# Mixture attention: VectorE's maxima one head ahead, ScalarE's exponentials ahead of the high halves

## The chip, the cores and the metric

One core of a Trainium2 chip runs the whole program. The metric is the device time of that core in microseconds (us), from launch to end; the profile's span, from the first instruction to the last, is a little shorter.

## The reference

A two-layer decoder over 8 batches of 256 tokens of width 256: layer 0 is a gated cross attention, then a gated mixture-attention layer; layer 1 a gated cross attention, then a mixture of 12 experts. The change touches only the mixture attention:

```python
q = einsum('btc,hdc->bhtd', x, Wq);  k = einsum('btc,hdc->bhtd', x, Wk)      # 16 heads of 64
w, sel = top_k(einsum('btc,hec->bthe', x, Ws), 2)                            # 2 of 8 value experts
mix_v = one-hot(sel) weighted by sigmoid(w)
v = einsum('bthe,bted->bhtd', mix_v, einsum('btc,edc->bted', x, Wv))
attn = softmax(q @ k.T / 8) @ v                                              # per batch and head
mask_o = two-hot of top_k(einsum('btc,hec->bthe', x, Wd), 2)                 # 2 of 8 output experts
res = einsum('bthe,bthd,efd->btf', mask_o, attn, Wo)
```

x is layer-normed first, and the result is added to x with a gate. No causal mask, so a head's scores are 256 x 256.

## The kernel before, in words

Every engine runs one instruction stream in order and meets the others at counting semaphores. Matrix products are taken in fp16 with each factor split into a high and a low half (three products, `matmul3`, lines 82 to 84). Splitting a product that lies in PSUM takes two engines: ScalarE copies the high half out, then VectorE subtracts it and writes the low half, which frees the bank.

The stage (`ffn_stage`, line 899) walks 8 batches b with 16 steps h each (one head a step), and a drain of 16 steps. In step h of batch b:

- TensorE (line 1326): transposes of the exponentials of head h-1 (L1225), value products of head h-3, one *product* of the next batch's front (`project(b + 1, h)`), then `score(b, h + 2)`. After the score, at steps 9 and 12 it does the mix-back of the batch before (`mixed_back`, L1309), and at 11 and 14 its output product. The front's products are, by step: 0 the transposes of x, 1 the gates, 2 and 3 the expert values, 4 to 10 and 15 queries and keys in turn, 11 to 14 the mixed values.
- ScalarE (line 1181): the high half of the transposed exponentials of head h-2 (`pt_part`), the high half of the product of step h-1 (`high`), then the exponentials of head h (`exps`, L1154), and in odd steps the normalising of a finished pair of heads (`normalise`). At step 4 it also converts the heads' outputs (`heads_hi`), at steps 10 and 13 the high half of a mix-back (`back_hi`).
- VectorE (line 1478): the maxima of head h (`maxima`, L1437), at h = 0 the normalised x of the next batch, the low half of `pt_part`, in odd steps reciprocals of row sums, the low half of the product of step h-1 (`low`, `low_x`), and then the extras: gate choice in five parts (steps 2 to 6), the heads' low halves (step 4), the spread of output masks (7, 8), of mixed values (10 to 13), low halves of the mix-back (10, 13), updates of x (12, 15).

Two score banks S alternate by head. `score(n)` waits until the exponentials of head n-2 have left its bank; `maxima(n)` waits for `score(n)` and for the exponentials of n-2, whose maxima it overwrites; `exps(n)` waits for `maxima(n)` and for the transposes of n-2. Two more banks hold, in turn, everything of the front, the mix-back and the output product, in the order that `bank_uses` lists; each use waits (`open_bank`, line 1257) until the use two before it has been released by VectorE. The gates product waits for the low half of x.

The other stages, among them the cross attentions and the experts, are not touched. GpSimd and SP serve the stage with row copies and DMA round trips.

Of the kernel before, what the change touches and what calls it, by code (L numbers as in the profile page):

```python
# [35 lines left out]
B, SQ, D = 8, 256, 256  # L36
SK = 120
H = 16
# [855 lines left out]
def at_head(h):  # L894

    return h % H8, h // H8


def ffn_stage(nc, a, s):
# [7 lines left out]
    with ExitStack() as ctx:  # L907
# [65 lines left out]
        def earlier(b, h, lag, do):  # L973

            if h >= lag and b < B:
                do(b, h - lag)
            elif h < lag and b >= 1:
                do(b - 1, h - lag + H)
# [138 lines left out]
        @block.scalar  # L1117
        def _(act):
            def pt_part(b, h):
                n = H * b + h  # L1120
                act.wait_ge(pt_ready, n + 1)
                if n >= 2:
                    act.wait_ge(pv_done, n - 1)
                act.activation(pt[h % 2][:, 0].rearrange("p c t q -> p (c t q)"), PT(h), ACT.Copy,  # L1124
                               scale=SPLIT).then_inc(pt_hi, 1)

            def high(b, j):
                use = b, FF_ORDER[j]
                what, r = use[1]
                act.wait_ge(front_ready, USE[use] + 1)  # L1130
                front = bank(use)
                if what == F_XN:
                    ins = act.activation(xt[b % 2][:, 0].rearrange("p c q -> p (c q)"), front, ACT.Copy, scale=SPLIT)
                elif what == F_GATES:
                    act.activation(g[:].rearrange("p a e -> p (a e)"), front, ACT.Copy, scale=UNSPLIT)
                    act.activation(mix[:], front.rearrange("p (t v h e) -> p t v h e", t=TPB, v=2, h=H)[:, :, 0],
                                   ACT.Exp, scale=-UNSPLIT).then_inc(act_high, 1)
                    return
                else:
                    if what == F_PV and r == 0 and b >= 1:  # L1140
                        act.wait_ge(pv_out, 16 * b)
                    if what == F_MIXV and r % 2 == 0 and b >= 1:
                        act.wait_ge(v_out[r // 2], 16 * b)
                    to, _, scale = parts_of(use)
                    ins = act.activation(to, front.rearrange("p (a c) -> p a c", a=to.shape[1]), ACT.Copy, scale=scale)
                ins.then_inc(act_high, 1)

            def exps(b, h):
                n = H * b + h
                act.wait_ge(s_max, n + 1)  # L1150
                if n >= 2:
                    act.wait_ge(pt_ready, n - 1)
                for ti in range(TPB):
                    ins = act.activation(pr[h % 2][:, ti, :], S(h)[:, ti, :], ACT.Exp, bias=nb[h % 2][:, ti:ti + 1])  # L1154
                ins.then_inc(p_ready, 1)

            def normalise(b, hp):
                h = 2 * hp
                act.wait_ge(rs_done, H // 2 * b + hp + 1)
                for i in range(2):  # L1160
                    h8, x = at_head(h + i)
                    for ti in range(TPB):
                        ins = act.activation(at[:, ti, h8, x, :], O(h)[:, i, ti, 0:DH], ACT.Copy,
                                             scale=rs[hp % 2][:, 2 * i + ti:2 * i + ti + 1])
                ins.then_inc(o_done, 1)

            def heads_hi(b, ti):
                act.wait_ge(o_done, H // 2 * (b + 1))
                if b >= 1:
                    act.wait_ge(at_out[ti], 16 * b)  # L1170
                act.activation(at_row[:, ti, :, 0:DH], at[:, ti].rearrange("p h x d -> p (h x) d"), ACT.Copy).then_inc(at_hi, 1)

            def back_hi(b, ti):
                use = b, (F_Z, ti)
                act.wait_ge(front_ready, USE[use] + 1)
                act.activation(zt[:, 0].rearrange("p c q -> p (c q)"), bank(use), ACT.Copy).then_inc(act_high, 1)

            act.wait_ge(made, 6)
            for j in range(FF_FRONT - 1):
                high(0, j)  # L1180
            for b in range(B + 1):
                for h in range(H):
                    earlier(b, h, FF_LAG - 1, pt_part)
                    was = (b, FF_FRONT - 1) if h == 0 else (b + 1, h - 1)
                    if was[0] < B:
                        high(*was)
                    for ti in range(TPB):
                        if b >= 1 and h == SPLIT_STEPS[ti]:
                            back_hi(b - 1, ti)
                        if b >= 1 and h == HEADS_STEPS[ti]:  # L1190
                            heads_hi(b - 1, ti)
                    if b < B:
                        exps(b, h)
                    if h % 2 == 1:
                        if h >= 5 and b < B:
                            normalise(b, (h - 5) // 2)
                        elif h < 5 and b >= 1:
                            normalise(b - 1, (h - 5) // 2 + H // 2)
# [148 lines left out]
        def _(dve):  # L1347
# [53 lines left out]
            def spread_values(b, r):  # L1401

                if r == 0:
                    dve.wait_ge(mix_in, 16 * (b + 1))
                if r >= 2:
                    dve.wait_ge(front_ready, USE[b, (F_MIXV, r - 2)] + 1)
                elif b >= 1:
                    dve.wait_ge(front_ready, USE[b - 1, (F_MIXV, r + 2)] + 1)
                n = SPREAD * 4
                dve.tensor_tensor(spread_v[r % 2][:].rearrange("p g l t h -> p (g l) t h"),  # L1410
                                  mix_in_t[:, SPREAD * r:SPREAD * r + SPREAD].rearrange("p g l h -> p (g l) h")
                                  .unsqueeze(2).to_broadcast([P, n, TG, H8]),
                                  same[:].unsqueeze(1).to_broadcast([P, n, TG, H8]), ALU.mult).then_inc(v_spread, 1)
# [54 lines left out]
            for j in range(FF_FRONT - 1):  # L1468
                if j == 0:
                    low_x(0)  # L1470
                low(0, j)
                if j == 1:
                    dve.wait_ge(act_high, HIGH[0, (F_GATES, 0)] + 1)
                if j in GATE_STEPS:
                    gate_choice(GATE_STEPS.index(j))
                if j + 1 in VALUE_STEPS:
                    spread_values(0, VALUE_STEPS.index(j + 1))
            for b in range(B + 1):
                for h in range(H):
                    if b < B:  # L1480
                        maxima(b, h)
                    if h == 0 and b < B - 1:
                        normalised_x(b + 1)
                    earlier(b, h, FF_LAG - 1, pt_part)
                    if h % 2 == 1:
                        if h >= 5 and b < B:
                            reciprocals(b, (h - 5) // 2)
                        elif h < 5 and b >= 1:
                            reciprocals(b - 1, (h - 5) // 2 + H // 2)
                    if h == 0 and b < B:  # L1490
                        low(b, FF_FRONT - 1)
                    if h >= 1 and b < B - 1:
                        if h == 1:
                            low_x(b + 1)
                        low(b + 1, h - 1)
                    if b >= 1:
                        for ti in range(TPB):
                            if h == HEADS_STEPS[ti]:
                                heads_lo(b - 1, ti)
                            if h == MASK_STEPS[ti]:  # L1500
                                spread_masks(b - 1, ti)
                            if h == SPLIT_STEPS[ti]:
                                back_lo(b - 1, ti)
                            if h == UPDATE_STEPS[ti]:
                                update(b - 1, ti)
                    if b < B - 1:
                        if h == GATE_STEPS[0]:
                            dve.wait_ge(act_high, HIGH[b + 1, (F_GATES, 0)] + 1)
                        if h in GATE_STEPS:
                            gate_choice(GATE_STEPS.index(h))  # L1510
                        if h in VALUE_STEPS:
                            spread_values(b + 1, VALUE_STEPS.index(h))
# [667 lines left out]
```

## Time and profile before

| | |
|---|---|
| runs | 1353.25, 1360.85, 1361.38 us; median 1360.85 |
| profiled execution | 1361.75 us, span 1360.0 us, mean granted TensorE clock 0.933 |
| TensorE busy | 1154.2 us, 85% |
| VectorE busy | 1102.8 us, 81% |
| ScalarE busy | 884.4 us, 65% |
| GpSimd busy | 357.3 us, 26% |

The shares are means over stages with different limits. The mixture attention lies between 262 and 690 us, the part of it before that being the first batch's front, and the drain after it runs to some 710 us. TensorE's busy time counts pipelined matmuls with modelled ends, so that a busy TensorE is not one at its peak. The granted clock is given as a share of full speed.

### The profile page before, as it was taken

What the parts mean: (1) busy time and instruction counts of PE and PEld (TensorE: products, weight loads), DVE (VectorE), ACT (ScalarE), POOL (GpSimd) and SP (SyncE); (2) the same over time, 40 slices, a digit from 0 to 9 for tenths busy, and PEclk for the clock granted to TensorE, in tenths of its full rate; (3) what the DMA queues carried; (4) which work ended last, traced back from release to release, by engine and by line L of the source; (5) the groups of instructions that cost most, each with busy time, mean ns of one, the idle gap of its engine ahead of it and who ended that gap; (6) DMA issues with size and microseconds to landing.
All of it is one profiled execution on the core that took longest, in us unless ns stands there. A gap on an engine that the chain in (4) does not pass through costs nothing. (4 is left out here: it accounts for less than half of the span.)

```text
span 1360.0 us, 34641 instructions
## 1 busy us (share of the span) xinstructions
PE 1154.2 (85%) x13183; PEld 942.7 (69%) x13183; DVE 1102.8 (81%) x2341; ACT 884.4 (65%) x2039; POOL 357.3 (26%) x346
## 2 busy tenths in 40 slices
PE   2678876798999989899976877757999999999996
PEld 2367664576867867677644766644689889999895
DVE  5578886699999999999644898868698888888884
ACT  1388883377767767677633888842567777767772
POOL 2312210000000000000004222101166676666763
PEclk8899997899999999999798899856899999999999
DMA  8122210315343352353322222106688888878870
GB/s 245 44 76 73 58 45 16 91 46 159 81 106 114 86 146 70 106 134 88 87 67 64 61 65 69 33 1 203 213 250 242 242 241 235 235 234 231 232 208 10
DMA packets 214082, 170.31 MB, mean 125 GB/s; under 512 B 87965, under 2 KB 196402, under 8 KB 213922
## 3 DMA queue, kind: packets, MB, share of 16 engines
q1 hardware_dynamic: 193922, 146.89, 36.3%
q0 software_dynamic: 13936, 16.79, 6.3%
q10 hardware_dynamic: 6064, 4.46, 1.1%
q8 instruction: 106, 1.74, 0.5%
q14 instruction: 54, 0.44, 0.1%
HBM read 126.13 MB, written 42.86 MB: 124 GB/s over the span
## 5 line engine op out<-in xcount | busy, mean ns | idle before, releaser
L1966 POOL DMA_INDIRECT out<-m_yo,m_xg x70 | 161.2, 2303 | 134.9 <-DVE m_yo L2082 121.6
L1988 ACT ACTIVATE m_hf<-m_ps,m_bue 128x256 f32<-128x256 f32 x280 | 117.1, 470 | 107.2 <-PE m_ps L84 107.2
L1154 ACT ACTIVATE f_pr<-f_ps,f_nb 128x256 f32<-128x256 f32 x256 | 107.7, 476 | 71.0 <-DVE f_nb L1437 70.6
L82 PE MATMUL m_ps<-m_ds,m_hs 128*128 128x256 f16 x560 | 152.6, 273 | 0.3 <-DVE m_yo L2082 0.3
L82 PE MATMUL m_ps<-m_xt,m_us 128*128 128x256 f16 x560 | 152.7, 273 | 0.0
L83 PE MATMUL m_ps<-m_xt,m_us 128*128 128x256 f16 x560 | 152.6, 273 | 0.0
L84 PE MATMUL m_ps<-m_xt,m_us 128*128 128x256 f16 x560 | 152.6, 273 | 0.0
L84 PE MATMUL m_ps<-m_ds,m_hs 128*128 128x256 f16 x560 | 152.6, 273 | 0.0
L83 PE MATMUL m_ps<-m_ds,m_hs 128*128 128x256 f16 x560 | 152.6, 273 | 0.0
L707 PE MATMUL x_ps<-ident,x_pr 128*120 128x128 f32 x512 | 84.8, 292 | 41.0 <-DVE x_pt L785 32.0
L1645 DVE SCALAR_TENSOR_TENSOR m_ds<-m_draw,m_ds 128x2048 f16<-128x2048 f32 x35 | 80.2, 2291 | 41.5 <-ACT m_ds L1633 41.5
L1106 POOL CAST f_mix_row<-f_mix 128x256 f16<-128x256 f32 x8 | 5.1, 640 | 372.6 <-DVE f_mix L1373 372.6
L1441 DVE SCALAR_TENSOR_TENSOR f_pt<-f_ps,f_pt 128x512 f16<-128x512 f32 x128 | 87.3, 682 | 17.8 <-ACT f_pt L1124 17.7
L1592 POOL DMA_INDIRECT m_xg<-expert_in,m_row_of x70 | 83.4, 1191 | 69.5 <-DVE m_row_of L1905 40.8
L2072 DVE SCALAR_TENSOR_TENSOR m_hs<-m_hf,m_hs 128x512 f16<-128x512 f32 x140 | 96.9, 692 | 4.8
L707 PEld LDWEIGHTS x_ps<-ident,x_pr 128*120 128x120 f32 x512 | 59.6, 145 | 59.0 <-issue 34.7
L82 PE MATMUL f_ps<-f_kt,f_qt 64*128 64x256 f16 x256 | 71.4, 280 | 28.6 <-ACT f_pr L1154 28.4
L785 DVE SCALAR_TENSOR_TENSOR x_pt<-x_ps,x_pt 120x512 f16<-120x512 f32 x128 | 87.7, 685 | 8.1 <-ACT x_pt L620 7.6
L1124 ACT ACTIVATE f_pt<-f_ps 128x512 f16<-128x512 f32 x128 | 78.9, 617 | 19.9 <-PE f_ps L84 19.7
L611 ACT ACTIVATE x_pr<-x_neg,x_mx 128x120 f32<-128x120 f32 x256 | 80.1, 395 | 13.8 <-DVE x_mx L779 13.8
L1437 DVE TENSOR_REDUCE f_nb<-f_ps 128x2 f32<-128x512 f32 x128 | 87.3, 682 | 1.9 <-PE f_ps L84 0.7
L1225 PE MATMUL f_ps<-ident,f_pr 128*128 128x128 f32 x512 | 85.5, 291 | 0.0
(374 smaller groups left out, 3890.9 us busy)
## 6 DMA issues: line engine op xcount, KB each, us to landing
m_uraw<-in_L_ffn_Wup SPq DMA_DIRECT2D x35, 1024.0 KB, 5.4
m_draw<-in_L_ffn_Wdown SPq DMA_DIRECT2D x35, 1024.0 KB
head_values<-f_v_row SPq DMA_DIRECT2D x16, 520.0 KB, 5.0
f_vh<-head_values SPq DMA_DIRECT2D x16, 520.0 KB, 3.6
head_outputs<-f_at_row SPq DMA_DIRECT2D x16, 512.0 KB, 3.8
f_at_in_t<-head_outputs SPq DMA_DIRECT2D x16, 512.0 KB, 5.3
x_q_stack<-x_queries SPq DMA_DIRECT2D x48, 128.0 KB, 2.8
x_queries<-x_qt SPq DMA_DIRECT2D x16, 256.0 KB, 2.4
```

Source lines behind the costliest of these rows:

```text
L82: pe.matmul(out, lhs[0], rhs[0], start=(n == 0), stop=False)
L83: pe.matmul(out, lhs[0], rhs[1], start=False, stop=False)
L84: last = pe.matmul(out, lhs[1], rhs[0], start=False, stop=(n == len(terms) - 1))
L707: last = pe.transpose(PT(u)[:, h, :], pr[u % 2][:, h, :], s.ident[:])
L785: dve.scalar_tensor_tensor(pt[u % 2][:, 1], PT(u), SPLIT, pt[u % 2][:, 0], ALU.mult, ALU.subtract).then_inc(pt_done, 1)
L1154: ins = act.activation(pr[h % 2][:, ti, :], S(h)[:, ti, :], ACT.Exp, bias=nb[h % 2][:, ti:ti + 1])
L1225: last = pe.transpose(PT(h)[:, at_:at_ + P], pr[h % 2][:, ti, c * P:(c + 1) * P], s.ident[:])
L1437: dve.tensor_reduce(nb[h % 2][:], S(h), AX_X, ALU.max, negate=True).then_inc(s_max, 1)
L1441: dve.scalar_tensor_tensor(pt[h % 2][:, 1].rearrange("p c t q -> p (c t q)"), PT(h), SPLIT, pt[h % 2][:, 0].rearrange("p c t q -> p (c t q)"),
L1966: pool.indirect_dma_start(rows_of, bass.IndirectOffsetOnAxis(xg[j % RING][:, ti, D:D + 1].bitcast(I32), 0), yo[j % 2][:, ti, :], None, bou ...
L1988: ins = act.activation(hf[:, q, m, :], U(q)[:, m, :], ACT.Gelu, bias=weights.bue[par][:, 2 * q + m:2 * q + m + 1], scale=UNSPLIT)
L2072: dve.scalar_tensor_tensor(hs[par][:, 1, 2 * q:2 * q + 2, :], hf[:, q], SPLIT, hs[par][:, 0, 2 * q:2 * q + 2, :], ALU.mult, ALU.subtract). ...
```

## The change

The edits are in two loops of `ffn_stage`. In ScalarE's, `exps(b, h)` moves up in the step, ahead of `high`, `back_hi` and `heads_hi`. In VectorE's, `maxima(0, 0)` runs once ahead of the loop, and step n of the loop begins with the maxima of head n+1 where it began with those of n; the last step has none. Nothing else changes: the buffers, the semaphores and their counts stay.

```diff
@@ ScalarE's loop
                     earlier(b, h, FF_LAG - 1, pt_part)
+                    if b < B:
+                        exps(b, h)
                     was = (b, FF_FRONT - 1) if h == 0 else (b + 1, h - 1)
                     if was[0] < B:
                         high(*was)
...
                         if b >= 1 and h == HEADS_STEPS[ti]:
                             heads_hi(b - 1, ti)
-                    if b < B:
-                        exps(b, h)
                     if h % 2 == 1:
@@ VectorE's loop
+            maxima(0, 0)
             for b in range(B + 1):
                 for h in range(H):
-                    if b < B:
-                        maxima(b, h)
+                    if H * b + h + 1 < H * B:
+                        maxima(b + (h + 1) // H, (h + 1) % H)
                     if h == 0 and b < B - 1:
                         normalised_x(b + 1)
                     earlier(b, h, FF_LAG - 1, pt_part)
```

## Rows read from the trace of the kernel before

**Rows 1.** The stage: us, then busy us (x instructions) by engine, PEclk, DMA, GB/s.
```profile
262.00:690.00 428.00, 393.98 (x5418) 309.35 (x5417) 390.13 (x657) 302.92 (x788) 16.38 (x42) 0.97 0.38 101
```
**Rows 2.** Waits in 262 to 690: who waits, for whom, total us, times, longest.
```profile
ACT f_pr L1154 <- DVE f_nb L1437: 70.6, 63, 3.1
...
PE f_ps L82 <- ACT f_pr L1154: 28.4, 34, 1.8
...
DVE f_pt L1441 <- ACT f_pt L1124: 17.7, 31, 1.7
```
**Rows 3.** Busy times as in rows 1, batch 2 from its step 2.
```profile
369.97:398.95 28.98, 25.93 (x257) 18.62 (x254) 27.23 (x43) 19.21 (x49) 2.34 (x6) 0.94 0.58 146
398.95:400.82 1.87, 1.87 (x27) 1.53 (x26) 1.87 (x5) 1.15 (x5) 0.00 (x0) 1.00 0.13 11
400.82:405.02 4.20, 4.20 (x100) 3.55 (x99) 3.70 (x6) 3.39 (x10) 0.00 (x0) 1.00 0.02 4
405.02:408.02 3.00, 3.00 (x53) 2.41 (x52) 3.00 (x6) 2.77 (x9) 0.00 (x0) 1.00 0.02 5
408.02:412.15 4.13, 4.13 (x89) 3.67 (x90) 4.03 (x9) 2.38 (x5) 0.00 (x0) 1.00 0.01 2
412.15:415.74 3.59, 3.17 (x92) 2.75 (x84) 3.59 (x7) 2.83 (x9) 0.00 (x0) 1.00 0.20 61
...
417.54:420.93 3.39, 3.39 (x40) 2.93 (x40) 3.04 (x8) 2.70 (x9) 0.00 (x0) 1.00 0.41 118
...
423.38:425.53 2.15, 2.15 (x31) 1.70 (x27) 1.95 (x6) 1.91 (x6) 0.00 (x0) 1.00 0.04 8
...
388.00:391.50 3.50, 3.50 (x22) 2.20 (x19) 3.40 (x7) 2.00 (x5) 0.00 (x0) 0.52 1.19 272
```
**Rows 4.** ScalarE in order of time, steps 9 and 10: start, us, instruction, [idle before].
```profile
399.67 0.84 ACT L1154 ACTIVATE f_pr<-f_ps,f_nb 128x256 f32<-128x256 f32 x2 [1.12 <-DVE f_nb L1437]
400.39 0.93 ACT L1163 ACTIVATE f_at<-f_ps,f_rs 128x64 f32<-128x64 f32 x4
...
401.65 0.64 ACT L1145 ACTIVATE f_kt<-f_ps 128x512 f16<-128x512 f32 x1
```
**Rows 5.** TensorE in order of time: score of step 2, step 9, product 13, transposes of x.
```profile
371.60 0.28 PE L82 MATMUL f_ps<-f_kt,f_qt 64*128 64x256 f16 x1
...
398.39 0.66 PE L1225 MATMUL f_ps<-ident,f_pr 128*128 128x128 f32 x4
...
399.25 0.27 PE L82 MATMUL f_ps<-f_xt,fk 128*128 128x256 f16 x1
...
400.66 0.28 PE L82 MATMUL f_ps<-f_kt,f_qt 64*128 64x256 f16 x1
...
401.41 1.20 PE L1309 MATMUL f_ps<-f_spread_z,f_at_in_t 128*64 128x64 f16 x64
...
414.24 0.19 PE L82 MATMUL f_ps<-f_pv_in_t,f_spread_v 128*128 128x64 f16 x1 [0.42 <-DVE f_v_row L1390]
...
415.03 0.28 PE L82 MATMUL f_ps<-f_kt,f_qt 64*128 64x256 f16 x1
...
423.37 0.63 PE L1274 MATMUL f_ps<-ident,f_xn 128*128 128x128 f32 x4
```
**Rows 6.** VectorE in order of time: gate choice, mask spread, step 13, normalised x.
```profile
372.61 0.29 DVE L1355 TENSOR_SCALAR f_mix<-f_mix 128x256 f32<-128x256 f32 x1 [0.71 <-ACT f_mix L1136]
...
397.82 1.21 DVE L1422 TENSOR_TENSOR f_spread_z<-f_mask_in_t,f_same_t 128x2048 f16<-128x2048 f16 x1
...
412.15 0.68 DVE L1437 TENSOR_REDUCE f_nb<-f_ps 128x2 f32<-128x512 f32 x1
...
413.34 0.17 DVE L1449 RECIPROCAL f_rs<-f_ps 128x4 f32<-128x4 f32 x1
413.43 0.66 DVE L1390 SCALAR_TENSOR_TENSOR f_v_row<-f_ps,f_v_row 128x512 f16<-128x512 f32 x1
...
421.54 0.73 DVE L1397 TENSOR_SCALAR f_xn<-x,mv,rstd 128x256 f32<-128x256 f32 x2
```

## Prediction

> **What bounds the kernel now.** The changed loops run only in the mixture-attention stage, so I first cut the span to it: 262 to 690 us, 428.0 us, with VectorE busy 390.1, TensorE 394.0, ScalarE 302.9 [rows 1]. Two engines are above 90%, so the question is which of them waits, and where. The list of waits [rows 2] is what speaks for the change: ScalarE's exponentials stood 70.6 us, 63 times, waiting for VectorE's maxima, and TensorE stood 28.4 us, 34 times, waiting for those exponentials, which free the two score banks. But a wait is only worth what the waiting engine does with it, so I then took one batch step by step [rows 3]. The batch from 369.97 to 425.53 us has two halves. In steps 2 to 8 VectorE has the gate choice, the low halves of the heads and the mask spreads: busy 27.2 of 29.0 us, TensorE 25.9; here VectorE is the bound, and the waits on the maxima fall here. From step 9 to step 1 TensorE has no gap in the rows shown but the 0.42 in step 13, while VectorE idles 0.5 in step 10, 0.35 in step 15 and 0.2 in step 1. There TensorE is the bound and VectorE runs just behind it. The batch is thus a relay of two bounds, 55.56 us.
>
> **The change part by part.** No instruction is added or dropped; no DMA is issued elsewhere, and the queues of SP and GpSimd keep their order. What is new is what stands behind which wait.
>
> (a) ScalarE: exponentials ahead of the high half (and, in steps 4, 10 and 13, ahead of the heads' or mix-back's high half). The exponentials of step n now run before the high half of the previous product, which they delay by one pair, 0.72 us [rows 4]. Its readers are VectorE's low half and, through that, TensorE.
>
> (b) VectorE: maxima one head ahead. The maxima of head n+1 stand first in VectorE's step n. They need the scores of n+1, which TensorE issues at the end of its step n-1, behind the product of that step. Before, the first work of step n needed the scores of n, one whole TensorE step older. So VectorE can no longer enter step n before TensorE has ended step n-1, and behind this new wait stand, in its queue, the pt low half, the reciprocal and the low half that frees TensorE's bank.
>
> That low half is late for whom? The banks of products alternate between two. As a rule TensorE's product n waits for the low half that VectorE does in step n-1, which leaves a step of slack. But the mix-back and output products take turns in the same two banks at steps 9, 11, 12 and 14, so products 10, 12, 13 and 15 and the mix-back of step 9 wait for the low half of the *same* step; and the gates product (step 1) waits for the low half of x in VectorE's step 1, the transposes of x (step 0) for VectorE's normalisation in step 0. For those the wait closes a serial loop: score, maxima, pt, low half, product, score.
>
> Prices, from rows. Score start to the maxima behind it: 0.75 to the next TensorE instruction [rows 5], 0.07 that the last matmul's end lies beyond, and a hand-over of some 0.05: 0.88 (estimate; 0.75 to 0.95). VectorE from the start of a step to the end of the low half: 412.15 to 414.09, 1.94 in an odd step, 0.09 less in an even one without the reciprocal; the product of step 13 began at 414.24, a hand-over of 0.15 [rows 5, 6]. So product n starts 2.09 (odd) or 2.00 (even) after VectorE's step. TensorE from step start to product 0.86 (transposes of P and value products), a 12-matmul product 1.41 (399.25 to 400.66; output products are 12 such, 1.32), a mixing product 0.79, mix-back 1.13, transposes of x 0.56, score 0.75 [rows 5].
>
> **The walk from step 9 to the gate choice**, time 0 being VectorE's step 9 (398.95). TensorE comes in early, since the exponentials no longer hold it: its product 9 needs only the low half of step 8, which ends 0.08 into the mask spread of 397.82, so it starts at 397.82+0.08+0.15, that is -0.90 (before: 399.25, +0.30). That is the gain of the change, 1.2 us. Then:
> Step 9: score 0.51; mix-back ready 1.26, waits for the low half to 2.09, ends 3.22.
> Step 10: VectorE enters at 1.87. ScalarE normalises from 1.44 (400.39), is past pt high at 2.70 (401.65), exponentials 0.72, high half 0.64 [rows 4]: 4.06. The low half is so 1.0 later than VectorE's own time and ends 4.75; product ready 4.08, starts 4.90; score 6.31. VectorE is through at 6.42 and must wait for the score: step 11 at 7.19.
> Step 11: product 7.92, score 8.71, output 9.46 to 10.78. VectorE step 12 at 10.19.
> Step 12: product ready 11.64, starts 12.19; score 12.98; mix-back to 14.86. VectorE step 13 at 10.19+4.13 = 14.32 [rows 3].
> Step 13: ready 15.72, starts 16.41; score 17.20. VectorE through at 17.91, step 14 at 18.08.
> Step 14: product 18.81, score 19.60, output to 21.67. VectorE step 15 at 20.48.
> Step 15: product 22.57, score 23.98. VectorE through after its 3.04 at 23.52, step 0 at 24.86.
> Step 0: transposes of x ready 25.59; normalised x is there at 24.86+0.61+0.73+0.15 = 26.35 [rows 6]; score 26.91. VectorE step 1 at 27.79.
> Step 1: gates product ready 28.52, x's low half there at 29.88; score 31.29. VectorE step 2 at 32.17, gate choice behind maxima and pt low half (1.21) at 33.38.
> Before, that point lay at 26.58 (to 425.53) + 2.64 (369.97 to 372.61 [rows 6]) = 29.22. **Loss 4.2 us a batch**: 1.9 up to the transposes of x (24.42 before), 1.2 more to the gates product, 1.1 more because the gate choice (1.01 after the score's start before, 371.60 to 372.61) now stands behind maxima that wait for that score. Steps 2 to 8 stay as they are, VectorE-bound without a wait: there the exponentials come earlier and nothing follows from it.
>
> Seven batches (0 to 6) pass these steps: 7 x 4.2 = 29.4. Batch 0 has no mix-back, but is bound by TensorE earlier; batch 6 has no x behind it; I leave the two as alike. Batch 7 has no projections: in its odd steps the normalise and pt high (1.26) and the exponentials (0.84) now sit in the loop from score to maxima, while the exponentials of step 4 no longer wait behind the heads' high halves. I bound it by those 2.1 us: -2 (one such stretch gone) to +4 (a quarter of it in each of eight odd steps), and take 0, since the rows decide for neither. Sum +29.4 on a profiled time of 1361.75 (span 1360.0; 0.9 above the median 1360.85): **1390** against the median. Bounds: with 0.75 for the hand-over the seven waits a batch shrink by 0.13 each, -6 in all; with 0.95, +3; batch 7 -2 to +4. The forecast's own range is 1380 to 1400.
>
> **The rivals.**
> *Faster.* If TensorE's scores are always there before VectorE asks, the new wait costs nothing and VectorE loses its idle time: 28.98-27.23 = 1.75 in steps 2 to 8, 0.5+0.1+0.35+0.2 in the steps after [rows 3], 2.9 a batch, 20 over seven: 1341. It decides at one place, the entry into steps 11, 14, 15, 0 and 1: it needs TensorE to end step n-1 before VectorE ends its own. For it: in steps 2 to 8 it does. Against: from step 9 on TensorE already runs without a gap, so it can't be early there. Chance 0.12.
> *No change.* The 70.6 us are ScalarE's, which is busy 71%; if VectorE's entry is later but only the x and gates steps feel it (1.2+1.1 a batch) and TensorE's early start of 1.2 holds through step 15, 1.1 a batch is left, +8, 1369. For it: my walk loses that lead in the waits of steps 9, 10, 12 and 13, each under 1 us and each hanging on a hand-over of a tenth. The Trainium skill (Perfetto Trace Analysis, Optimization Strategy) would have one look for the gaps of the most-contended engine and start what they wait for sooner. By that rule ScalarE's 70.6 us are the wrong gaps, and the time would stay at 1361. Chance 0.14.
> *Slower still, by the clock.* TensorE's clock shows 0.52 in 388.0 to 391.5, right behind the step in which it waited longest [rows 3]; there it costs nothing, VectorE being the bound. With waits of 0.5 to 1.4 us in seven steps of a batch it may fall from 2.4 to 1.2 GHz in steps 9 to 1, where TensorE is in the loop: 3.5 us at half speed cost 1.75, one a batch +12, 1402. The Trainium skill (TensorE: Matmul & The Clock Gate, A second HAM failure mode) says that short idling between matmul groups makes the gate oscillate and lowers throughput; by that rule this case is likelier than by the rows, where the clock in steps 9 to 1 is 1.00 throughout. Chance 0.14.
> That the change does not do what it says can be left out: both moves are orders of queues.
>
> **How the numbers follow.** Forecast 0.60, faster 0.12, no change 0.14, clock 0.14. Predicted 1390. The range 1360 to 1402 leaves out the faster case and the upper half of the clock's. About 1% (1347 to 1374) is what a measurement can tell from no change: faster 0.12; within 0.17 (the no-change case and 0.03 of the forecast, if steps 9 to 13 cost half); slower 0.71.
>
> **What would show it.** A batch of 59.7 us between the maxima of step 2, against 55.56; waits of VectorE's maxima on TensorE's scores, one before and some 35 to 45 after, together over 25 us; ScalarE's wait on maxima near zero; TensorE waiting for low halves and x, 4 to 5 us a batch; TensorE busy 87% or less in the stage; stage 262 to about 719. I am wrong if the step-2-to-step-2 distance is under 57, if those maxima don't wait at steps 11, 14, 15, 0, 1 and 2, or if the half clock shows in steps 9 to 1.

## Result: slower, and the profile after

The changed kernel took 1395.59 us (median of four runs, 1385.75 to 1397.18) against 1357.05 for the kernel before (1352.50 to 1361.38): a ratio of 1.0247, 95% interval 1.0193 to 1.0301. The forecast was 1390, its range 1360 to 1402. By the medians the change costs 38.5 us. The forecast had added its 29.4 us to a median of 1360.85, which with a fourth run is 1357.05, so the total is closer to the mark than the loss is. The profiled execution took 1397.18 us; its span is 1395.5, 35.5 longer than before.

The engines' busy times and three groups of instructions, from the page of the changed kernel: the maxima, the normalising and the exponentials, with busy us and mean ns, then the idle time before them and what ended most of it. They answer to [rows 2]:

```profile
PE 1168.5 (84%) x13183; PEld 952.1 (68%) x13183; DVE 1103.9 (79%) x2341; ACT 881.7 (63%) x2039; POOL 357.9 (26%) x346
...
L1437 DVE TENSOR_REDUCE f_nb<-f_ps 128x2 f32<-128x512 f32 x128 | 88.0, 688 | 52.7 <-PE f_ps L84 49.5
L1163 ACT ACTIVATE f_at<-f_ps,f_rs 128x64 f32<-128x64 f32 x256 | 59.4, 316 | 110.9 <-DVE f_rs L1449 110.1
...
L1154 ACT ACTIVATE f_pr<-f_ps,f_nb 128x256 f32<-128x256 f32 x256 | 110.3, 500 | 2.2 <-DVE f_nb L1437 2.2
```

The change did what it says: ScalarE's exponentials waited 70.6 us for maxima before and 2.2 after. VectorE and ScalarE have no more work (busy 1.1 us more and 2.7 less); TensorE is busy 14.3 us more with the same matmuls, at a mean granted clock of 0.924 for 0.933. What is new is idle time, 49.5 us of VectorE's maxima behind TensorE's scores, and ScalarE now waits for reciprocals instead. The waits of the changed kernel between 262 and 725 us (who waits, for whom, total, times, longest):

```profile
ACT f_at L1163 <- DVE f_rs L1449: 110.1, 55, 3.4
DVE f_nb L1437 <- PE f_ps L84: 49.5, 46, 4.3
...
PE f_ps L1225 <- DVE f_pt L1441: 25.0, 27, 2.5
...
PE f_ps L82 <- DVE f_xt L1379: 7.5, 7, 1.2
...
PE f_ps L82 <- DVE f_v_row L1390: 5.5, 12, 0.5
PE f_ps L1274 <- DVE f_xn L1397: 5.5, 7, 1.9
...
PE f_ps L82 <- ACT f_pr L1154: 4.0, 4, 1.3
```

Which of these cost time is read from one batch. Batch 2 of the changed kernel, from the gate choice of step 2 through steps 9 to 15, 0 and 1 to the next gate choice; columns as in [rows 1], steps as in [rows 3]:

```profile
384.19:410.54 26.35, 21.58 (x232) 16.14 (x231) 25.87 (x41) 16.63 (x42) 2.34 (x6) 1.00 0.51 134
410.54:412.41 1.87, 1.56 (x14) 0.97 (x11) 1.87 (x6) 0.47 (x3) 0.00 (x0) 1.00 0.14 13
412.41:417.64 5.23, 4.43 (x99) 3.70 (x100) 3.79 (x6) 4.47 (x12) 0.00 (x0) 1.00 0.02 3
417.64:420.64 3.00, 3.00 (x53) 2.60 (x54) 3.00 (x5) 1.58 (x6) 0.00 (x0) 1.00 0.02 5
420.64:424.77 4.13, 3.70 (x88) 3.21 (x87) 4.03 (x8) 2.88 (x7) 0.00 (x0) 1.00 0.00 2
424.77:428.53 3.76, 3.27 (x89) 2.80 (x84) 3.69 (x8) 2.95 (x9) 0.00 (x0) 1.00 0.25 70
428.53:430.94 2.41, 2.41 (x47) 2.08 (x48) 1.89 (x3) 1.68 (x5) 0.00 (x0) 1.00 0.43 119
430.94:435.29 4.35, 4.35 (x47) 3.61 (x47) 2.96 (x7) 3.14 (x9) 0.00 (x0) 1.00 0.70 206
435.29:438.20 2.91, 2.30 (x27) 1.75 (x27) 2.53 (x5) 1.82 (x4) 0.00 (x0) 1.00 0.24 64
438.20:442.57 4.37, 3.19 (x35) 2.48 (x36) 1.96 (x5) 2.91 (x9) 0.00 (x0) 1.00 0.74 152
442.57:443.77 1.20, 1.20 (x19) 0.95 (x20) 1.20 (x2) 0.30 (x2) 0.00 (x0) 1.00 0.00 0
```

The first row, gate choice to step 9, is 26.35 us; before it was 398.95-372.61 = 26.34. So steps 2 to 8 lost nothing, and the waits that lie there (9.1 us of ScalarE's 15.3 for reciprocals in this batch, all 4.8 of TensorE's for `pt`) cost nothing there. All is lost in the rows after it: 33.23 us, against 29.22. VectorE's idle time there stands at the head of a step, as its timeline shows (start, us, instruction, idle time before it):

```profile
417.64 0.69 DVE L1437 TENSOR_REDUCE f_nb<-f_ps 128x2 f32<-128x512 f32 x1 [0.61 <-PE f_ps L84]
...
430.94 0.69 DVE L1437 TENSOR_REDUCE f_nb<-f_ps 128x2 f32<-128x512 f32 x1 [0.53 <-PE f_ps L84]
...
435.29 0.69 DVE L1437 TENSOR_REDUCE f_nb<-f_ps 128x2 f32<-128x512 f32 x1 [1.32 <-PE f_ps L84]
...
438.20 0.69 DVE L1437 TENSOR_REDUCE f_nb<-f_ps 128x2 f32<-128x512 f32 x1 [0.37 <-PE f_ps L84]
...
442.57 0.69 DVE L1437 TENSOR_REDUCE f_nb<-f_ps 128x2 f32<-128x512 f32 x1 [2.41 <-PE f_ps L84]
```

TensorE, without a gap before but for 0.42 [rows 5], now waits six times, each time for a half, or for normalised x, that VectorE does behind the maxima of the same step (TensorE's timeline, the rows with idle time):

```profile
412.63 1.20 PE L1309 MATMUL f_ps<-f_spread_z,f_at_in_t 128*64 128x64 f16 x64 [0.53 <-DVE f_qt L1390]
415.36 0.28 PE L82 MATMUL f_ps<-f_xt,fq 128*128 128x256 f16 x1 [0.57 <-DVE f_kt L1390]
...
422.68 0.19 PE L82 MATMUL f_ps<-f_pv_in_t,f_spread_v 128*128 128x64 f16 x1 [0.43 <-DVE f_v_row L1390]
...
426.87 0.19 PE L82 MATMUL f_ps<-f_pv_in_t,f_spread_v 128*128 128x64 f16 x1 [0.49 <-DVE f_v_row L1390]
...
436.77 0.63 PE L1274 MATMUL f_ps<-ident,f_xn 128*128 128x128 f32 x4 [0.61 <-DVE f_xn L1397]
...
440.30 0.27 PE L82 MATMUL f_ps<-fg,f_xt 128*128 128x256 f16 x1 [1.18 <-DVE f_xt L1379]
```

Not all six stand right behind a wait of the maxima. The last two do (steps 0 and 1). In step 9 VectorE did not wait: TensorE came early. In step 10 it waited 0.31 us for ScalarE's part of `pt` and 0.53 for the high half, which stands behind the moved exponentials. In steps 12 and 13 it ran without idle time, but late since its 0.61 at the head of step 11. So both engines wait for each other in turn. From gate choice to gate choice a batch takes 59.57 us instead of 55.56 (batches 1 to 5, all within 0.02). Against before, the stage enters 1.1 us later, ahead of the first moved instruction; steps 0 and 1 of batch 0 cost 3.3, batch 0 3.2, batches 1 to 5 20.1, batch 6 up to step 2 of batch 7 2.1, batch 7 with the drain 5.1: 34.9 of the span's 35.5.

### The profile page after: what moved, and what is told of

Same layout as the page of the kernel before. It is cut to its first block and busy times, and to the rows that moved or that the text cites. A ratio compares the mean times of both kernels' runs of the same rounds, so it can differ in the third digit from the quotient of the medians.

```text
span 1395.5 us, 34641 instructions
## 1 busy us (share of the span) xinstructions
PE 1168.5 (84%) x13183; PEld 952.1 (68%) x13183; DVE 1103.9 (79%) x2341; ACT 881.7 (63%) x2039; POOL 357.9 (26%) x346
## 5 line engine op out<-in xcount | busy, mean ns | idle before, releaser
L1437 DVE TENSOR_REDUCE f_nb<-f_ps 128x2 f32<-128x512 f32 x128 | 88.0, 688 | 52.7 <-PE f_ps L84 49.5
L1163 ACT ACTIVATE f_at<-f_ps,f_rs 128x64 f32<-128x64 f32 x256 | 59.4, 316 | 110.9 <-DVE f_rs L1449 110.1
L1225 PEld LDWEIGHTS f_ps<-ident,f_pr 128*128 128x128 f32 x512 | 57.8, 148 | 49.5 <-issue 47.1
```

The lines of the kernel that those rows point to most:

```text
L1225: last = pe.transpose(PT(h)[:, at_:at_ + P], pr[h % 2][:, ti, c * P:(c + 1) * P], s.ident[:])
L1437: dve.tensor_reduce(nb[h % 2][:], S(h), AX_X, ALU.max, negate=True).then_inc(s_max, 1)
```

## Experiments

The theory: the loss sits at the head of VectorE's step, where the low half, normalised x and x's low half queue behind maxima of a score that TensorE has only just issued. The rivals: ScalarE's half of the change does it; or the clock. The batch from gate choice to gate choice (55.56 before, 59.57 after) is the measure that runs vary least in.

**Each half alone.** `maxima_only` keeps VectorE's half and puts ScalarE's order back:

```diff
                     earlier(b, h, FF_LAG - 1, pt_part)
-                    if b < B:
-                        exps(b, h)
...
                             heads_hi(b - 1, ti)
+                    if b < B:
+                        exps(b, h)
```


> Only VectorE's half of the change; ScalarE keeps the exponentials behind the high halves. If VectorE's entry into a step waiting for the score is the cost, nearly all of it stays: about 1390 us, a batch (step 2 to step 2) of 58.6 to 59.0 against 59.57 with the whole change, since only the late low half of step 10 (0.8) goes. If ScalarE's order is the cost, the time falls back to about 1357 and the batch to 55.6.

Measured: 1386.64 us, ratio 1.0216 (1.0189 to 1.0243); batch 58.94, maxima waiting 52.2 us in 50 waits. So VectorE's half alone costs 3.4 of the 4.0 us, and ScalarE's order adds 0.6 to it.

`exps_only` keeps ScalarE's half:

```diff
-            maxima(0, 0)
...
-                    if H * b + h + 1 < H * B:
-                        maxima(b + (h + 1) // H, (h + 1) % H)
+                    if b < B:
+                        maxima(b, h)
```


> Only ScalarE's half; VectorE takes the maxima of head n in step n, as before. Theory: the exponentials then wait in front of the high half, which comes 0.8 later than VectorE's low half wants it in some 13 steps of a batch: 1410 to 1440 us, VectorE waiting for high halves 50 us or more in all. Rival, that earlier exponentials are worth something by themselves: 1357 or less.

Measured: 1435.32 us, ratio 1.0564 (1.0530 to 1.0597); batch 66.22. The waits of this kernel between 262 and 740 us:

```profile
ACT f_pr L1154 <- DVE f_nb L1437: 181.8, 100, 3.3
...
DVE f_v_row L1390 <- ACT f_v_row L1145: 22.3, 29, 1.3
...
DVE f_qt L1390 <- ACT f_qt L1145: 19.7, 28, 0.7
```

The same fault on the other queue: the exponentials, moved forward, wait 181.8 us for maxima that are not there yet, and the high halves behind them are late for VectorE, which waits 70.1 us for them in the four kinds of product (50 or more were expected). ScalarE's half needs VectorE's; the whole loss is not the sum of the halves.

**Which wait.** `x_first` is the whole change with normalised x ahead of the maxima in step 0:

```diff
-                    if H * b + h + 1 < H * B:
-                        maxima(b + (h + 1) // H, (h + 1) % H)
                     if h == 0 and b < B - 1:
                         normalised_x(b + 1)
+                    if H * b + h + 1 < H * B:
+                        maxima(b + (h + 1) // H, (h + 1) % H)
```


> The whole change, but in step 0 VectorE normalises x before the maxima that wait, not behind them. Theory: TensorE no longer waits for x in step 0, the batch is 0.6 to 0.8 shorter (58.8 to 59.0), total 5 less, about 1390. Rival, that the entry wait costs nothing there because something else is late: 59.5.

Measured: 1381.94 us (one run); batch 58.78, that is 0.79 less. The one work taken from behind the wait came back as expected; the rest of the loss stayed. The total is 8 us under the expected 1390, about half of it from the last batches (below).

`score_first` gives VectorE its scores earlier instead: TensorE does the score ahead of the product.

```diff
-                    if b < B - 1:
-                        project(b + 1, h)
...
+                    if b < B - 1:
+                        project(b + 1, h)
```
(out of its place ahead of `score`, and in again right behind it)

> The whole change, and TensorE issues the score of a step ahead of its product instead of behind it. Theory: VectorE's entry wait then ends 1.4 us earlier (a product), low halves come before they are wanted, and the lead of TensorE is kept: a batch of 53 to 54.5 against 55.56 before, 1335 to 1350 us, maxima waiting under 10 us in all. Rival, that the loss comes from the two shared banks or from ScalarE's order: 1385 or more, a batch of 58 or more.

Measured: 1370.82 us, ratio 1.0092 (1.0071 to 1.0113); batches of 56 and 57 us in turn. The direction was right, 2.6 to 3.6 of the 4.0 came back, but the expected gain over the kernel before did not come. Its waits between 262 and 725 us:

```profile
ACT f_at L1163 <- DVE f_rs L1449: 62.8, 54, 3.1
...
PE f_ps L82 <- ACT f_pr L1154: 22.0, 24, 1.4
...
DVE f_nb L1437 <- PE f_ps L84: 16.8, 36, 2.4
```

The maxima wait 16.8 instead of 49.5, and TensorE waits for exponentials 22.0 instead of 4.0: a score moved forward asks for its bank sooner. `score_first_old`, the same edit on the kernel before, shows that side alone:

> The kernel before with TensorE's score ahead of its product, and nothing else. The score of a step then asks for exponentials that ScalarE does behind the high half of a product that has just ended: a wait of some 0.6 us in each step of 9 to 1, a batch of 60 or more, 1390 to 1415 us. If instead the order of score and product is worth something by itself: at or under before.

Measured: 1415.53 us, ratio 1.0414 (1.0372 to 1.0455); batch 62.2 to 63.7, TensorE waiting 73.9 us for exponentials in 95 waits. So score first is dear by itself and worth something only where the maxima are already ahead.

**Where the maxima may stand.** `maxima_late` is the whole change, but VectorE takes the maxima of n+1 in the middle of step n, behind the low half that TensorE needs and ahead of the extras:

```diff
-                    if H * b + h + 1 < H * B:
-                        maxima(b + (h + 1) // H, (h + 1) % H)
...
                         low(b + 1, h - 1)
+                    if H * b + h + 1 < H * B:
+                        maxima(b + (h + 1) // H, (h + 1) % H)
```


> The same place for the maxima, with ScalarE's exponentials ahead of the high halves. Theory: in the steps without extras the exponentials now stand right behind maxima that are just done and hold the high half back, as in the run of ScalarE's half alone but in 5 to 8 steps of a batch: a batch of 57 to 61, 1370 to 1395 us. Rival, that ScalarE's order is free once the maxima are early: as the run with the old order.

Measured: 1370.78 us, ratio 1.0088 (1.0055 to 1.0121); batch 56.76, just under the 57 to 61 expected. `maxima_late_exps_old` has the same place for the maxima and ScalarE's order of before:

> The maxima of head n+1 stand in VectorE's step n behind the low half of the product and ahead of the extras (gate choice, spreads, updates); ScalarE's order is the old one. In steps without extras this is the old order, so nothing new waits in steps 9 to 1; in steps 2 to 8 the exponentials come earlier and TensorE enters step 9 with more lead. Theory: a batch of 54.3 to 55.4 against 55.56, total 1 to 9 us under before; VectorE's maxima wait under 5 us in all. Rival, that any maxima ahead of their old place cost: a batch over 56.

Measured: 1352.40 us (twelve runs), ratio 0.9932 (0.9911 to 0.9953); batch 55.13. This version beats both kernels. Its waits between 262 and 700 us:

```profile
ACT f_pr L1154 <- DVE f_nb L1437: 16.2, 16, 1.3
...
PE f_ps L82 <- ACT f_pr L1154: 11.3, 22, 1.8
...
DVE f_nb L1437 <- PE f_ps L84: 6.2, 8, 1.8
```

ScalarE's 70.6 us shrink to 16.2, TensorE's 28.4 to 11.3, and the maxima wait 6.2 us instead of 49.5 (under 5 were expected). Even so 54.4 us fewer of ScalarE's waits bring 0.43 us a batch. The pair also prices ScalarE's order by itself, with the maxima in a good place: 56.76-55.13 = 1.6 us a batch, since the high halves stand behind exponentials that still wait 42.4 us for maxima in `maxima_late`.

`low_first` tried to take more: in that version TensorE still waits 0.53 us ahead of the mix-back of step 9 and 0.39 in step 13 for low halves, so in these two steps `low` went ahead of `pt_part`.

```diff
+                    if h in (9, 13) and b < B - 1:
+                        low(b + 1, h - 1)
                     earlier(b, h, FF_LAG - 1, pt_part)
...
-                        low(b + 1, h - 1)
+                        if h not in (9, 13):
+                            low(b + 1, h - 1)
```


> The version with the maxima behind the low half and ScalarE's old order, and in steps 9 and 13 VectorE does the low half of the product ahead of the low half of pt. Those are the two steps in which TensorE still waits, 0.53 for the low half before the mix-back and 0.39 before a mixing product, in a stretch that it otherwise fills. Theory: a batch of 54.2 to 54.8 against 55.13, total 3 to 6 us under that version, about 0.8 to 1.1% under before. Rival, that TensorE's stretch is bound again right behind (by the gates product): 55.1.

Measured: 1358.00 us, ratio 1.0012 (0.9985 to 1.0040); batch 55.57, 0.44 worse. A miss, and the trace shows the step. ScalarE, then VectorE and TensorE of `low_first` in steps 9 and 10 of batch 2, each from its own timeline:

```profile
401.54 0.93 ACT L1163 ACTIVATE f_at<-f_ps,f_rs 128x64 f32<-128x64 f32 x4 [1.58 <-DVE f_rs L1449]
```
```profile
402.99 0.69 DVE L1441 SCALAR_TENSOR_TENSOR f_pt<-f_ps,f_pt 128x512 f16<-128x512 f32 x1 [0.91 <-ACT f_pt L1124]
```
```profile
404.33 0.28 PE L82 MATMUL f_ps<-f_xt,fq 128*128 128x256 f16 x1 [1.15 <-DVE f_kt L1390]
```

In `maxima_late_exps_old` the first of these had waited 0.98:

```profile
400.86 0.93 ACT L1163 ACTIVATE f_at<-f_ps,f_rs 128x64 f32<-128x64 f32 x4 [0.98 <-DVE f_rs L1449]
```

The mix-back's wait is gone (401.03, right behind the score), but the reciprocals of step 9 came 0.6 later with `pt_part`. ScalarE's normalise waits for them, and its high halves of step 10 stand behind that; VectorE's low half of the product of step 9 is later, and TensorE's product of step 10 waits 1.15 instead of nothing. By product 13, whose wait is gone, TensorE has made up all but 0.05 us, but VectorE is still 0.6 late, and in step 14 TensorE waits for its spread of mixed values (0.21 us, new), which leaves it 0.42 behind.

**The last batch.** `last_batch_old` is the whole change in batches 0 to 6, with the maxima of batch 7 in their old place:

```diff
-                    if H * b + h + 1 < H * B:
+                    if H * b + h + 1 < H * (B - 1):
...
+                    if b == B - 1:
+                        maxima(b, h)
```


> The whole change in batches 0 to 6; in batch 7 VectorE takes the maxima in their own step, as before. Gate choice of batch 6 to the end of the stage took 117.5 us before and 124.8 with the change. If the maxima ahead cost 5 us in batch 7: 117.5 to 119.5, total about 1388. If it was the stretch of half clock (13.7 us before, 27.3 with the change), which falls as it will: anything from 118 to 125, total 1388 to 1396, and the stretch tells which.

Measured: 1389.33 us, ratio 1.0219 (1.0186 to 1.0252); batch 59.57 as in the changed kernel, and from the gate choice of batch 6 to the end of the stage 118.91 us instead of 124.76. `after_again` ran the changed kernel once more, to see whether its last batch is always so:

> The changed kernel once more, unchanged. The batch is an order of waits and comes out at 59.5 to 59.6 again. The end, from the gate choice of batch 6 to the end of the stage, took 124.8 us with 27.3 us at half clock; if the clock is what it hangs on, it is 119 to 122 where the half clock is 13 to 18 us, and the total about 1388 to 1392. If the maxima ahead cost it, it is 124 to 125 again at whatever clock.

Measured: 1391.10 us, ratio 1.0231 (1.0186 to 1.0276); batch 59.57, last stretch 124.49. That stretch, from the gate choice of batch 6 to the end of the stage, one row each of the kernel before, the changed one, `maxima_only`, `last_batch_old`, `maxima_late_exps_old` and `low_first` (columns as in [rows 1]; the granted clock is third from the end):

```profile
594.83:712.35 117.52, 101.40 (x1396) 76.27 (x1395) 88.46 (x158) 70.70 (x185) 2.38 (x7) 0.93 0.32 89
```
```profile
622.48:747.24 124.76, 105.71 (x1379) 79.38 (x1378) 88.47 (x158) 69.06 (x183) 2.38 (x7) 0.88 0.29 83
```
```profile
618.67:738.79 120.12, 100.47 (x1379) 75.91 (x1378) 88.36 (x158) 69.26 (x183) 2.39 (x7) 0.93 0.31 86
```
```profile
621.18:740.09 118.91, 100.18 (x1379) 75.90 (x1378) 88.31 (x158) 69.56 (x183) 2.38 (x7) 0.93 0.31 87
```
```profile
594.23:713.37 119.14, 103.71 (x1391) 77.91 (x1388) 87.90 (x158) 70.28 (x184) 2.38 (x7) 0.89 0.31 87
```
```profile
596.07:706.66 110.59, 93.39 (x1391) 71.27 (x1387) 87.15 (x158) 69.57 (x184) 2.38 (x7) 1.00 0.34 93
```

The last two have the same order in batch 7, and differ by 8.55 us with the clock: 0.89 means 119.14 x 0.11 x 2 = 26.2 us at the lower level, so about a third of a microsecond for each of them. By that the changed kernel's 29.9 us against 16.5 before are worth 4.4 of its extra 7.2 (an estimate). At the clock of before, 0.93, `maxima_only` lost 2.6 and `last_batch_old` 1.4, so the order itself looks like the smaller part.

The two runs made for the question do not settle it: 118.91 us for `last_batch_old` fits both readings set down for it, and `after_again` had the clock of the changed kernel again, 0.88. `x_first` says more: its edit acts for the last time in step 0 of batch 6, so from there on it has the order of the changed kernel. It took 120.78 us in that stretch, also at 0.88, but a part of its time at the lower clock fell into batch 6. From step 2 of batch 7 to the end, the kernel before, the changed one and `x_first`:

```profile
647.17:712.35 65.18, 52.50 (x704) 37.77 (x701) 38.31 (x76) 34.09 (x92) 0.04 (x1) 0.90 0.27 78
```
```profile
676.95:747.24 70.29, 58.03 (x688) 41.56 (x689) 38.23 (x74) 33.76 (x92) 0.04 (x1) 0.78 0.25 72
```
```profile
669.81:735.17 65.36, 52.13 (x689) 37.35 (x690) 38.10 (x75) 33.70 (x92) 0.04 (x1) 0.85 0.27 77
```

With the same order, and a clock below that of the kernel before, `x_first` took 0.2 us more than the kernel before, the changed kernel 5.1. So little of the 5.1 is the order's; most of it goes with the clock. This rests on one run, and no run held the clock fixed.

## Why the prediction was right, point by point

**The relay of two bounds** held. Steps 2 to 8 took 26.34 us before and 26.35 after, while most of the waits that the change removed lay there. That the 70.6 us of ScalarE were worth next to nothing left the new waits to set the sign; `maxima_late_exps_old` shows it from the other side, with 54.4 us of them gone for 0.43 a batch.

**The walk** held step by step. From VectorE's step 9 it put the steps 11, 12, 13, 14, 15, 0, 1 and 2 at 7.19, 10.19, 14.32, 18.08, 20.48, 24.86, 27.79 and 32.17, and the gate choice at 33.38. Measured: 7.10, 10.10, 14.23, 17.99, 20.40, 24.75, 27.66, 32.03 and 33.23. Of the 0.15 at the end 0.09 is there by step 11. TensorE's starts agree too: mix-back 2.09 for 2.09, product 10 4.82 for 4.90, normalised x's transposes 26.23 for 26.35, gates 29.76 for 29.88. Its early start of product 9 was 0.66 us ahead of VectorE's step, not 0.90 (its transposes had waited 0.42 for `pt`, which the walk left out); nothing hung on it, since the mix-back waits for the low half of the same step either way. The batch came out at 59.57 for 59.7.

**The waits** came where they were named: 46 of the maxima, 49.5 us, for "35 to 45, together over 25"; TensorE's six in a batch add up to 3.81, just under the 4 to 5 forecast. TensorE's share of 262 to 690 us is 373.24 of 428, 87%. ScalarE's 110.1 us behind the reciprocals had not been named. In steps 9 to 1 of batch 2 they are 6.2 us, and what VectorE waited there for ScalarE is 0.84, in step 10, which the walk had.

**The sum** was right by terms that partly cancel. Seven passes of 4.2 made 29.4; they cost 3.2 (batch 0), 20.1 (five batches) and 2.1 (batch 6), 25.4. "I leave the two as alike" was the step that failed there: the short batches lose less. Steps 0 and 1 of batch 0, which also have x and the gates product behind the new wait, were left out and cost 3.3, and the entry 1.1. Batch 7, taken as 0 within -2 to +4, cost 5.1, beyond its bound: the bound counted ScalarE's work in the loop, not the clock. So the end of the stage moved by 34.9 and not 29.4, and the time came to 1395.59 and not 1390. The mechanism and the loss of a batch were understood; that the total came within 6 us is in part luck, of these terms and of the lower median before.

**The rivals.** Faster failed at the place named for it, the entry into steps 11, 15, 0 and 1, where VectorE waited 0.37 to 1.32 us; into step 14 it came some 0.1 late (428.45, the end of the spread, to 428.53), where the walk had 0.17. No change failed with the walk. The Trainium skill (Perfetto Trace Analysis, Optimization Strategy) advises to look for the gaps of the most-contended engine. The case bears it out so far that ScalarE's gaps were the wrong ones; that the time would stay at 1361, as the prediction read it, did not come true, since the change opened gaps on TensorE and VectorE.

The clock did not fall where the rival had it: it is 1.00 in all of steps 9 to 1 above, and in those of batches 1 to 5, with TensorE's six short waits among them. The Trainium skill (TensorE: Matmul & The Clock Gate, A second HAM failure mode) tells of a kernel in which frequent short idling between groups of matmuls makes the clock gate go to and fro; in steps 9 to 1 the trace does not show that. The clock did fall in batch 7, which the rival had not named.

## What to carry to other kernels

A wait is worth what ends last behind it: ask of each wait which engine bounds that stretch before counting its microseconds as gain. On an in-order queue an instruction moved forward brings its wait along, and everything behind it pays; place it behind the last work that another engine is waiting for, ahead of the work nobody waits for. Here, with ScalarE's order of before, that turned +3.4 us a batch (`maxima_only`) into -0.4 (`maxima_late_exps_old`). Count the first and the last pass of a loop by themselves: here they were 8.4 of 34.9 us, part of it the clock's.

## What the hardware showed unexpectedly

The granted clock in the last batch differed between kernels and between executions of like order, and moved the time as much as a whole edit. In the changed kernel TensorE waited 1.20, 0.98, 1.32 and 0.52 us for exponentials between 679 and 691 us, and ran at 0.50 of full speed, 1.2 GHz for 2.4, from 686 on:

```profile
686.00:700.00 14.00, 12.77 (x90) 9.30 (x91) 9.78 (x16) 7.92 (x25) 0.00 (x0) 0.50 0.56 161
700.00:713.00 13.00, 13.00 (x139) 9.94 (x138) 5.67 (x11) 5.73 (x17) 0.00 (x0) 0.50 0.00 1
713.00:727.00 14.00, 13.05 (x203) 9.66 (x201) 8.46 (x18) 11.06 (x30) 0.00 (x0) 0.99 0.01 2
```

The second of these rows has TensorE busy throughout and still at the lower level. The waits alone do not decide it: in batch 7 `low_first` and `maxima_late_exps_old` have the same order, and in each TensorE waited 0.4 and then 1.82 us; the one stayed at 1.00, the other went to 0.50 for some 20 us. What makes the difference is open.

`maxima_late_exps_old`, with waits of 0.53 and 0.39 us in each batch, kept 1.00 from 262 to its gate choice of batch 6 at 594.23; the kernel before had 0.98 up to 594.83. Its gain of 8.4 us over the kernel before (1352.40 for 1360.76) is more than the 3.0 us that its batches show in the profile (gate choice of batch 0 to that of batch 6: 322.62 for 325.58); that execution, the slowest of its twelve with 1360.82 us, had the long stretch at the lower clock. The rest goes with the clock as far as the record shows: its twelve executions have a mean granted clock of 0.944, the seventeen of the kernel before 0.937, and from its slowest to its fastest the clock goes from 0.937 to 0.951. Whether the order causes that is open.
